# Adding the causal mask of a row-maximum pass on VectorE instead of TensorE

## The chip, the cores and the metric

The kernel runs on one core of a Trainium2 chip. The metric is the device time of one execution in microseconds (us). A core has five engines with a queue each: TensorE (PE in the profile; its weight loads are listed apart as PEld), VectorE (DVE), ScalarE (ACT), GpSimd (POOL) and SyncE (SP), which here issues the DMAs. Engines wait for each other through semaphores.

## The reference, cut to what matters

The reference is two transformer layers over `x` of shape (2, 1024, 1024): attention, a mixing layer, attention, and a layer with a mixture of experts. The change lies in the two attentions, which compute the same apart from how the rotary pairs are formed:

```python
scores = jnp.einsum('bqhd,bkhd->bhqk', q, k) / np.float32(np.sqrt(HEAD_DIM))
mask = jnp.triu(jnp.full((seq_len, seq_len), -jnp.inf, dtype=scores.dtype), k=1)
scores = scores + mask
attn = jax.nn.softmax(scores.astype(jnp.float32), axis=-1).astype(q.dtype)
out = jnp.einsum('bhqk,bkhd->bqhd', attn, v).reshape(bsz, seq_len, N_HEADS * HEAD_DIM)
```

There are 32 query heads of 32 dimensions and 8 key/value heads, so 8 groups of 4 query heads. The sequence is 1024 long.

## The kernel before

`attention` handles one layer. For each of 2 batches it normalises and transposes `x`, projects keys, values and queries, and then works through the 8 head groups. In each group it makes the scores twice.

The **first pass** only finds each query's largest score, since the softmax is taken relative to it. Its work is cut into 38 uses (`USES`), each of which fills up to one PSUM bank of 512 columns: 8 tiles of 128 queries (`qt`), against one or two chunks of 512 keys (`kc`). A use is marked `last` when it holds the diagonal block. Then its width `n` is 128, 256, 384 or 512, and the two narrow widths put 4 or 2 heads side by side in a bank. 16 uses are not `last` (one head, 512 columns each). 22 are: 2 of four heads, 4 of two heads, 8 of one head with 384 columns and 8 of one head with 512.

For a use, `row_scores` (TensorE) waits until the bank is free, issues a score matmul per head (L738) and, in a `last` use, a second matmul per head (L743) that adds a 128x128 mask onto the last 128 columns: identity times a bf16 tile `negmask`, which holds 0 on and under the diagonal and -1e30 above. `maximum` (VectorE, L597) waits for the scores, takes one reduction over the whole bank with a result per head into `mx`, and frees the bank. Two banks of `psh` are used in turn, by `bank_plan`, so a use's scores wait for the maximum two uses earlier. At the end (`MT`) the maxima are merged, transposed on TensorE and stored to DRAM, from where the next group's second pass takes them as a 97th row of the queries.

The **second pass** (`ST`, L789) makes the transposed scores per unit of 128 keys by up to 512 queries, ScalarE takes the exponential (L502), GpSimd zeroes what the mask hides (L436), and TensorE multiplies by values and by ones (`PV`, L809). `NORM` on VectorE takes a reciprocal (L641, 3.35 us) and multiplies.

The order on every engine is written out by `iteration`: in the body for group g the second pass of g is interleaved with the query projection for g + 2 (`P`, L717) and the first pass of g + 1 (`S`, spread over the units 1 to 9). TensorE executes in that order, and VectorE takes its part of the same order: the maxima, the rotation after a projection (L580 to L585), the low parts (L590, L551) and `NORM`. The first group's first pass stands in `prologue`, among projections. So each batch of each layer has one first pass in the prologue and seven in the bodies; the last group's body has none.

Around the change, from the iteration's order (each step is issued as it stands):

```
ST 2,0  ST 2,1  S0  PV 1,0  S1  PV 1,1  S2  ST 3,0  S3  ST 3,1  PV 2,0  S4  PV 2,1  S5 ...
```

Of the kernel before, what the change touches and what calls it, by code (L numbers as in the profile page):

```python
# [16 lines left out]
BF16 = mybir.dt.bfloat16  # L17
ALU = mybir.AluOpType
ACT = mybir.ActivationFunctionType
AX = mybir.AxisListType  # L20

P = 128
# [8 lines left out]
BANK = 512  # L31
# [6 lines left out]
MASKED = -1e30  # L38
# [31 lines left out]
USES = score_uses()  # L70
# [119 lines left out]
def attention(nc, sem, layer, x_in, wqkv, cos_in, sin_in, swap, oT_d):  # L190
# [7 lines left out]
    s = {n: sem(f"a{layer}_{n}") for n in (  # L198
        "const", "table", *(f"xf{i}" for i in range(NX_BUF)), *(f"xl{i}" for i in range(NX_AHEAD)), "stats", "pow", "z_ready", "zT_ready", "zT_hi", "zT_evac",
        "wl0", "wl1", "w_hi", "w_ready", "sh_ready", "sh_free", "roped", "q_hi", "q_lo", "v_ready",  # L200
        "k_out", "q_out", "qs00", "qs01", "qs10", "qs11", "ks0", "ks1", "mx_ready", "mT_ready", "m_out", "mr0", "mr1", "st_ready",
        "exp_done", "mask_done", "pv_done", "acc_copied", "norm_done", "vg_ready", "os0", "os1",
        "pool_turn", "sp_turn", "pe_turn")}
    x_first, x_loaded = [s[f"xf{i}"] for i in range(NX_BUF)], [s[f"xl{i}"] for i in range(NX_AHEAD)]
    w_loaded = (s["wl0"], s["wl1"])
    max_row, o_stored = (s["mr0"], s["mr1"]), (s["os0"], s["os1"])
# [15 lines left out]
    with ExitStack() as ctx:  # L222
        def sb(name, shape, dt=F32):
            return ctx.enter_context(nc.sbuf_tensor(f"a{layer}_{name}", shape, dt))

        ident = sb("ident", [P, P])
        identb = sb("identb", [P, P], BF16)
        negmask = sb("negmask", [P, P], BF16)
        ones = sb("ones", [P, HD])
        nhalf = sb("nhalf", [P, 1])  # L230
        cos = sb("cos", [P, S])
# [185 lines left out]
        def _(pool):  # L417
# [26 lines left out]
                    copy_v(b, g + 2, par)  # L444

            pool.memset(ident[:, :], 0.0)
            pool.memset(negmask[:, :], 0.0)
            pool.memset(ones[:, :], 1.0)
            pool.memset(nhalf[:, :], -0.5)
            pool.drain()  # L450
            for i in range(2):
# [1 line left out]
            pool.drain()  # L453
            pool.affine_select(out=ident[:, :], in_=ident[:, :], compare_op=ALU.not_equal, fill=1.0, base=0,
                               pattern=[[-1, P]], channel_multiplier=1)
            pool.affine_select(out=negmask[:, :], in_=negmask[:, :], compare_op=ALU.is_ge, fill=MASKED, base=0,
                               pattern=[[-1, P]], channel_multiplier=1)
            pool.drain()
            pool.tensor_copy(identb[:, :], ident[:, :])
            pool.drain().then_inc(s["const"], 1)  # L460
            for k in range(ST_):
                reciprocal_deviation(k, k)
# [85 lines left out]
        def _(dve):  # L548
# [42 lines left out]
                    .then_inc(s["q_lo"], 1)  # L591

            def maximum(u, at, k):
                qt, kc, n, heads, _ = USES[k]
                m = len(heads)
                dve.wait_ge(s["sh_ready"], u + 1)
                dve.tensor_reduce(mx_hq[kc][:, heads[0]:heads[0] + m, qt],  # L597
                                  psh[:, at, 0:m * n].rearrange("p (m n) -> p m n", n=n), AX.X, ALU.max)\
                    .then_inc(s["sh_free"], 1)

            def max_rows(u, at):

# [103 lines left out]
        def _(pe):  # L706
# [25 lines left out]

            def row_scores(u, where, par, k):
                _, at, prev = where
                qt, kc, n, heads, last = USES[k]
                pe.wait_ge(s["sh_free"], SH0 + u + prev + 1)
                for i, h in enumerate(heads):
                    mm = pe.matmul(psh[:, at, i * n:(i + 1) * n], qst[par][0:96, h, qt * P:(qt + 1) * P],  # L738
                                   kst[par][0:96, kc * BANK:kc * BANK + n], start=True, stop=not last,
                                   skip_group_check=True)  # L740
                    if last:

                        mm = pe.matmul(psh[:, at, (i + 1) * n - P:(i + 1) * n], identb[:, :], negmask[:, :],  # L743
                                       start=False, stop=True, skip_group_check=True)
                mm.then_inc(s["sh_ready"], 1)

            def transpose_max(n, u, where):
# [1133 lines left out]
```

## Time and profile before

| quantity | value |
|---|---|
| median of 3 runs | 3196.64 us (3193.96 to 3196.96) |
| span of the profiled execution | 3192.5 us |
| median less span | 4.1 us |
| TensorE busy | 2861.6 us, 90% |
| VectorE busy | 2039.7 us, 64% |
| ScalarE busy | 1004.8 us, 31% |
| GpSimd busy | 282.5 us, 9% |

The profiled execution has no time of its own beside its span; the runs' times also hold what lies ahead of the first and after the last instruction. In the rows, L738 is line 738 of the kernel, `a_psh<-a_kst,a_qst` is what an instruction writes and reads, x48 is a count, and `<-DVE a_mx` behind an idle time names what ended it. A matmul's booked time includes its way through the array, so neighbouring ones overlap.

### The profile page before, as it was taken

The page shows a single profiled execution, that of the slowest core. Times are in us where ns is not written, and L with a number is a line of the kernel's source. Part 1 is how long each engine was busy: PE and PEld are TensorE (multiplying, and loading weights), DVE is VectorE, ACT ScalarE, POOL GpSimd, SP SyncE. Part 2 cuts the span into 40 slices and gives each one's busy share as a digit, 9 for nine tenths or more (in the row PEclk, how much of TensorE's full clock was granted, in tenths as well). Part 3 has the DMA queues.
Part 4 walks back from the last instruction along what each step waited for, and adds up shares of the span by engine and source line. Part 5 has one row for each costly group of instructions (what it writes and reads, how often), then busy time and mean ns, then how long its engine had stood idle before and what let it go on. Part 6 is the DMA issues. An engine that isn't in the chain of part 4 may idle for free. (4 is left out here: it accounts for less than half of the span.)

```text
span 3192.5 us, 48849 instructions
## 1 busy us (share of the span) xinstructions
PE 2861.6 (90%) x16848; PEld 1854.1 (58%) x16848; DVE 2039.7 (64%) x3303; ACT 1004.8 (31%) x1549; POOL 282.5 (9%) x397
## 2 busy tenths in 40 slices
PE   7999998999999799752869999989999997897999
PEld 6555454655554488642656555546555553786887
DVE  7676677767776433588776766767677774324443
ACT  2234334224334411252521433433234334201000
POOL 1011011001110000000010001011011110001111
PEclk9999999999999899875979999999999999998999
DMA  4322222323121322000133213213313120544111
GB/s 154 91 62 86 62 61 80 111 63 101 54 81 51 124 84 75 0 0 0 79 132 116 75 53 87 69 55 103 104 53 100 53 80 20 193 138 152 67 63 43
DMA packets 121063, 253.16 MB, mean 79 GB/s; under 512 B 12720, under 2 KB 39728, under 8 KB 120880
## 3 DMA queue, kind: packets, MB, share of 16 engines
q1 hardware_dynamic: 120912, 251.03, 24.8%
q8 instruction: 109, 1.79, 0.2%
q14 instruction: 42, 0.34, 0.0%
HBM read 166.57 MB, written 84.41 MB: 79 GB/s over the span
## 5 line engine op out<-in xcount | busy, mean ns | idle before, releaser
L597 DVE TENSOR_REDUCE a_mx<-a_psh 128x1 f32<-128x512 f32 (+3 forms) x1216 | 773.2, 660 | 351.5 <-PE a_psh L743 236.8
L502 ACT ACTIVATE a_prob<-a_pst 128x1024 f32<-128x1024 f32 (+3 forms) x768 | 595.9, 816 | 823.3 <-PE a_pst L789 821.0
L738 PE MATMUL a_psh<-a_kst,a_qst 96*128 96x512 f32 (+3 forms) x1536 | 543.6, 404 | 9.4 <-DVE a_mx L597 3.4
L738 PEld LDWEIGHTS a_psh<-a_kst,a_qst 96*128 96x128 f32 x1536 | 287.4, 192 | 396.8 <-DVE a_mx L597 327.4
L789 PE MATMUL a_pst<-a_qst,a_kst 97*128 97x512 f32 (+2 forms) x1536 | 424.3, 377 | 46.6 <-issue 17.5
L809 PE MATMUL a_ppv<-a_prob,a_vg 128*32 128x512 f32 (+3 forms) x3072 | 333.7, 507 | 12.5 <-POOL a_prob L436 11.1
L789 PEld LDWEIGHTS a_pst<-a_qst,a_kst 97*128 97x128 f32 x1536 | 256.6, 196 | 138.6 <-issue 72.3
L809 PE MATMUL a_pden<-a_prob,a_ones 128*32 128x512 f32 (+3 forms) x3072 | 329.9, 502 | 0.0
L436 POOL TENSOR_SCALAR_AFFINE_SELECT a_prob<-a_prob 128x512 f32<-128x512 f32 x256 | 178.6, 698 | 1383.7 <-ACT a_prob L502 1383.7
L641 DVE RECIPROCAL a_dens<-a_dens 128x512 f32<-128x512 f32 x64 | 214.6, 3353 | 68.2 <-ACT a_dens L510 55.2
L743 PE MATMUL a_psh<-a_negmask,a_identb 128*128 128x128 bf16 x1024 | 228.7, 232 | 0.0
L717 PE MATMUL a_psh<-a_xT_hi,a_w_hi 128*128 128x512 f32 x416 | 178.2, 428 | 2.6 <-issue 2.0
L717 PE MATMUL a_psh<-a_xT_lo,a_w_hi 128*128 128x512 f32 x416 | 168.2, 404 | 0.0
L1371 PE MATMUL h_pout<-h_w,h_o 128*128 128x512 f32 x720 | 167.7, 392 | 0.3 <-DVE h_x L1248 0.3
L717 PE MATMUL a_psh<-a_xT_hi,a_w_lo 128*128 128x512 f32 x416 | 167.5, 403 | 0.0
L743 PEld LDWEIGHTS a_psh<-a_negmask,a_identb 128*128 128x128 bf16 x1024 | 99.8, 97 | 93.9 <-issue 53.4
L1371 PEld LDWEIGHTS h_pout<-h_w,h_o 128*128 128x128 f32 x720 | 134.1, 188 | 28.2 <-DMA h_wb<-in_w_branch 0.7
L717 PE MATMUL a_pst<-a_xT_hi,a_w_hi 128*128 128x512 f32 x352 | 142.4, 404 | 6.7 <-DVE a_swp L581 4.5
L717 PE MATMUL a_pst<-a_xT_hi,a_w_lo 128*128 128x512 f32 x352 | 137.5, 391 | 0.0
L717 PE MATMUL a_pst<-a_xT_lo,a_w_hi 128*128 128x512 f32 x352 | 137.5, 391 | 0.0
L1454 PE MATMUL h_pout<-h_w,h_dg 128*128 x256 | 67.7, 411 | 61.9 <-ACT h_dg L1220 45.8
L809 PEld LDWEIGHTS a_pden<-a_prob,a_ones 128*32 128x32 f32 x3072 | 71.7, 110 | 82.7 <-issue 73.5
(213 smaller groups left out, 3786.8 us busy)
## 6 DMA issues: line engine op xcount, KB each, us to landing
a_qst<-q SPq DMA_DIRECT2D x192, 256.0 KB, 4.5
a_wraw<-in_wqkv SPq DMA_DIRECT2D x52, 512.0 KB, 5.6
q<-a_stg_hi SPq DMA_DIRECT2D x64, 256.0 KB, 2.5
q<-a_stg_lo SPq DMA_DIRECT2D x64, 256.0 KB, 2.8
oT<-a_oT SPq DMA_DIRECT2D x64, 256.0 KB, 2.5
a_kst<-kT SPq DMA_DIRECT2D x96, 128.0 KB, 3.0
h_oraw<-oT SPq DMA_DIRECT2D x16, 512.0 KB, 4.1
h_x<-in_x SPq DMA_DIRECT2D x16, 512.0 KB, 4.7
```

The lines of the kernel that those rows point to most:

```text
L436: pool.affine_select(out=blk, in_=blk, compare_op=ALU.is_ge, fill=0.0, base=0, pattern=[[0, GH], [1, P]], channel_multiplier=-1)\
L502: act.activation(prob[k % 2][:, 2 * half:2 * half + 2, off:], pst[:, half, :, off:], ACT.Exp, scale=scale).then_inc(s["exp_done"], 1)
L597: dve.tensor_reduce(mx_hq[kc][:, heads[0]:heads[0] + m, qt], psh[:, at, 0:m * n].rearrange("p (m n) -> p m n", n=n), AX.X, ALU.max)\
L641: dve.reciprocal(dens[:, :], dens[:, :])
L717: mm = pe.matmul(bank(at), w[par][a][:, k, :], xT[x][:, k, c * BANK:(c + 1) * BANK], start=(i == 0), stop=(i == len(passes) - 1))
L738: mm = pe.matmul(psh[:, at, i * n:(i + 1) * n], qst[par][0:96, h, qt * P:(qt + 1) * P], kst[par][0:96, kc * BANK:kc * BANK + n], start=Tru ...
L743: mm = pe.matmul(psh[:, at, (i + 1) * n - P:(i + 1) * n], identb[:, :], negmask[:, :], start=False, stop=True, skip_group_check=True)
L789: mm = pe.matmul(pst[:, half, hh, off:], kst[par][0:97, ki * P:(ki + 1) * P], qst[par][0:97, 2 * half + hh, qc * BANK + off:(qc + 1) * BAN ...
L809: mm = pe.matmul(acc[h * HD:(h + 1) * HD, off:], lhs, prob[k % 2][:, h, off:], start=(ki == 0), stop=(ki == 4 * qc + 3), skip_group_check= ...
L1371: mm = pe.matmul(pout[:, half, :], o[:, par, a, k, :], w[:, b, k, half * BANK:(half + 1) * BANK], start=(i == 0), stop=(i == len(passes) - 1))
L1454: mm = pe.matmul(pout[:, par, i * C:(i + 1) * C], dg[par][:, i * (NS + 1) + n, :], rhs, start=(n == 0), stop=(n == NS), skip_group_check=True)
```

## The change

VectorE adds the mask. In a `last` use, `maximum` issues one `tensor_tensor_reduce` per head: it adds the tile `edge` to the scores, writes the sums back over the scores in PSUM, and delivers the largest sum. `edge` is a bf16 tile of 512 columns, zeros with the triangle in its last 128 columns, so that its last n columns fit a use of width n. The mask matmuls, `negmask` and the bf16 identity `identb` go, with a drain and a cast at set-up. The wait of a `last` use is taken by a semaphore step on VectorE (`dve_turn`) ahead of its instructions. Other uses keep their reduction.

```diff
+        edge = sb("edge", [P, BANK], BF16)
-        identb = sb("identb", [P, P], BF16)
-        negmask = sb("negmask", [P, P], BF16)
...
+            pool.memset(edge[:, :], 0.0)
-            pool.affine_select(out=negmask[:, :], in_=negmask[:, :], compare_op=ALU.is_ge, fill=MASKED, base=0,
-                               pattern=[[-1, P]], channel_multiplier=1)
-            pool.drain()
-            pool.tensor_copy(identb[:, :], ident[:, :])
+            pool.affine_select(out=edge[:, BANK - P:], in_=edge[:, BANK - P:], compare_op=ALU.is_ge, fill=MASKED,
+                               base=0, pattern=[[-1, P]], channel_multiplier=1)
...
             def maximum(u, at, k):
-                qt, kc, n, heads, _ = USES[k]
+                qt, kc, n, heads, last = USES[k]
                 m = len(heads)
                 dve.wait_ge(s["sh_ready"], u + 1)
-                dve.tensor_reduce(mx_hq[kc][:, heads[0]:heads[0] + m, qt],
-                                  psh[:, at, 0:m * n].rearrange("p (m n) -> p m n", n=n), AX.X, ALU.max)\
-                    .then_inc(s["sh_free"], 1)
+                if last:
+
+                    dve.sem_inc(s["dve_turn"], 1)
+                    for i, h in enumerate(heads):
+                        scores = psh[:, at, i * n:(i + 1) * n]
+                        part = dve.tensor_tensor_reduce(scores, scores, edge[:, BANK - n:], 1.0, 2 * MASKED,
+                                                        ALU.add, ALU.max, mx_hq[kc][:, h, qt:qt + 1])
+                else:
+                    part = dve.tensor_reduce(mx_hq[kc][:, heads[0]:heads[0] + m, qt],
+                                             psh[:, at, 0:m * n].rearrange("p (m n) -> p m n", n=n), AX.X, ALU.max)
+                part.then_inc(s["sh_free"], 1)
...
             def row_scores(u, where, par, k):
                 for i, h in enumerate(heads):
                     mm = pe.matmul(psh[:, at, i * n:(i + 1) * n], qst[par][0:96, h, qt * P:(qt + 1) * P],
-                                   kst[par][0:96, kc * BANK:kc * BANK + n], start=True, stop=not last,
+                                   kst[par][0:96, kc * BANK:kc * BANK + n], start=True, stop=True,
                                    skip_group_check=True)
-                    if last:
-
-                        mm = pe.matmul(psh[:, at, (i + 1) * n - P:(i + 1) * n], identb[:, :], negmask[:, :],
-                                       start=False, stop=True, skip_group_check=True)
                 mm.then_inc(s["sh_ready"], 1)
```

## Rows read from the trace of the kernel before

**Rows 1.** The page: busy time by engine, and the chain that ended last.

```profile
PE 2861.6 (90%) x16848; PEld 1854.1 (58%) x16848; DVE 2039.7 (64%) x3303; ACT 1004.8 (31%) x1549; POOL 282.5 (9%) x397
...
PE 8%; DVE 1%; DMA 0%; issue 0%; DVEq 0%; SPq 0%; ACT 0%; POOL 0%
```

**Rows 2.** Windows: two head groups, the maxima's stretch, a prologue's maxima.

```profile
core 0: us, PE busy (x) PEld busy (x) DVE busy (x) ACT busy (x) POOL busy (x), PEclk, DMA share, GB/s
173.00:229.00 56.00, 55.84 (x377) 29.80 (x369) 41.05 (x58) 22.30 (x31) 6.41 (x9) 1.00 0.26 75
229.00:292.00 63.00, 58.47 (x373) 32.15 (x369) 40.67 (x57) 22.63 (x31) 5.55 (x9) 0.95 0.23 66
188.60:227.50 38.90, 38.74 (x271) 19.25 (x268) 26.96 (x44) 16.44 (x23) 3.64 (x5) 1.00 0.27 73
78.00:111.00 33.00, 29.42 (x146) 19.90 (x145) 28.08 (x45) 2.12 (x2) 0.74 (x2) 1.00 0.24 72
```

**Rows 3.** Groups by line, 188.6 to 227.5: count | busy, mean ns | idle before.

```profile
L597 DVE TENSOR_REDUCE a_mx<-a_psh 128x1 f32<-128x512 f32 (+3 forms) x38 | 24.2, 660 | 11.6 <-PE a_psh L743 7.7 <-PE a_psh L738 3.7
L738 PE MATMUL a_psh<-a_kst,a_qst 96*128 96x512 f32 (+3 forms) x48 | 17.1, 406 | 0.2
...
L738 PEld LDWEIGHTS a_psh<-a_kst,a_qst 96*128 96x128 f32 x48 | 9.0, 192 | 13.3 <-DVE a_mx L597 11.3 <-issue 1.6
```

**Rows 4.** The page's costliest groups: the mask matmuls.

```profile
L743 PE MATMUL a_psh<-a_negmask,a_identb 128*128 128x128 bf16 x1024 | 228.7, 232 | 0.0
```

**Rows 5.** Timeline of TensorE's matmuls: start us, us, then the instruction.

```profile
188.66 0.73 PE L789 MATMUL a_pst<-a_qst,a_kst 97*128 97x256 f32 x4
189.22 0.22 PE L738 MATMUL a_psh<-a_kst,a_qst 96*128 96x128 f32 x1
189.29 0.23 PE L743 MATMUL a_psh<-a_negmask,a_identb 128*128 128x128 bf16 x1
...
189.48 0.23 PE L743 MATMUL a_psh<-a_negmask,a_identb 128*128 128x128 bf16 x1
...
196.14 0.34 PE L738 MATMUL a_psh<-a_kst,a_qst 96*128 96x384 f32 x1
196.33 0.23 PE L743 MATMUL a_psh<-a_negmask,a_identb 128*128 128x128 bf16 x1
196.37 0.71 PE L789 MATMUL a_pst<-a_qst,a_kst 97*128 97x512 f32 x2
196.91 0.40 PE L738 MATMUL a_psh<-a_kst,a_qst 96*128 96x512 f32 x1
...
197.32 0.43 PE L809 MATMUL a_ppv<-a_prob,a_vg 128*32 128x128 f32 x8
...
214.17 0.40 PE L738 MATMUL a_psh<-a_kst,a_qst 96*128 96x512 f32 x1
...
214.88 0.40 PE L738 MATMUL a_psh<-a_kst,a_qst 96*128 96x512 f32 x1
215.21 1.06 PE L809 MATMUL a_ppv<-a_prob,a_vg 128*32 128x512 f32 x8
```

**Rows 6.** Groups by line and shape, whole span: the reductions.

```profile
L597 DVE TENSOR_REDUCE a_mx<-a_psh 128x1 f32<-128x512 f32 x768 | 510.3, 688 | 204.4 <-PE a_psh L738 105.1 <-PE a_psh L743 92.5
...
L597 DVE TENSOR_REDUCE a_mx<-a_psh 128x1 f32<-128x384 f32 x256 | 136.1, 553 | 69.8 <-PE a_psh L743 67.0
L597 DVE TENSOR_REDUCE a_mx<-a_psh 128x2 f32<-128x512 f32 x128 | 88.1, 691 | 59.8 <-PE a_psh L743 59.8
...
L597 DVE TENSOR_REDUCE a_mx<-a_psh 128x4 f32<-128x512 f32 x64 | 44.1, 689 | 17.5 <-PE a_psh L743 17.5
```

**Rows 7.** Timeline of VectorE at the start and near the end of the stretch.

```profile
190.97 1.28 DVE L597 TENSOR_REDUCE a_mx<-a_psh 128x4 f32<-128x512 f32 x2
192.96 0.69 DVE L597 TENSOR_REDUCE a_mx<-a_psh 128x2 f32<-128x512 f32 x1 [0.71 <-PE a_psh L743]
...
222.87 1.29 DVE L597 TENSOR_REDUCE a_mx<-a_psh 128x1 f32<-128x512 f32 x2 [0.37 <-PE a_psh L738]
```

**Rows 8.** Short and two-source VectorE work: groups by line, then a timeline.

```profile
L1352 DVE SCALAR_TENSOR_TENSOR h_x<-h_w,h_m,h_x x128 | 56.3, 481 | 18.0 <-issue 18.0
L581 DVE LOAD_MASK_SELECT a_swp<-a_psh x52 | 0.7, 14 | 0.0
...
2980.26 0.16 DVE L1652 TENSOR_REDUCE e_sc<-e_ge 128x1 f32<-128x8 f32 x1 [1.06 <-ACT e_ge L1602]
2980.34 0.14 DVE L1653 TENSOR_SCALAR e_sc<-e_ge 128x1 f32<-128x1 f32 x1
```

**Rows 9.** Waits, 78 to 111 us: us in total, times, longest.

```profile
DVE a_mx L597 <- PE a_psh L743: 2.8, 10, 0.4
```

**Rows 10.** Timeline of the start: GpSimd's last set-up step and TensorE's first matmuls.

```profile
4.16 0.29 POOL L459 CAST a_identb<-a_ident 128x128 bf16<-128x128 f32 x1
...
8.82 1.97 PE L729 MATMUL a_pst<-a_ident,a_xin 128*128 128x128 f32 x8 [8.82 <-DVE a_xin L566]
```

More of the change, by code:

```diff
@@ L202, in attention @@
         "exp_done", "mask_done", "pv_done", "acc_copied", "norm_done", "vg_ready", "os0", "os1",
-        "pool_turn", "sp_turn", "pe_turn")}
+        "pool_turn", "dve_turn", "sp_turn", "pe_turn")}
     x_first, x_loaded = [s[f"xf{i}"] for i in range(NX_BUF)], [s[f"xl{i}"] for i in range(NX_AHEAD)]
@@ L446, in _ @@
             pool.memset(ident[:, :], 0.0)
-            pool.memset(negmask[:, :], 0.0)
+            pool.memset(edge[:, :], 0.0)
             pool.memset(ones[:, :], 1.0)
@@ L734, in row_scores @@
                 _, at, prev = where
-                qt, kc, n, heads, last = USES[k]
+                qt, kc, n, heads, _ = USES[k]
                 pe.wait_ge(s["sh_free"], SH0 + u + prev + 1)
```

## The prediction

> **What bounds the kernel now.** I read the busy shares first, then the stretches by window, then the waits inside one stretch, then the timeline. TensorE is busy 90% of the span, VectorE 64% [rows 1]. The chain that ended last only covers the expert layer at the end [rows 1], so it says nothing of the attention; that has to be read by window. One head group of the attention takes 56.0 us and TensorE is busy 55.84 of them; in the 38.9 us in which the row maxima of the next group are made it is busy 38.74, at a granted clock of 1.00, with VectorE busy 26.96 [rows 2]. So TensorE's queue sets the time there. The waits seem to say otherwise: weight loads of the scores stand 11.3 us behind the maxima [rows 3]. But a PE matmul row has only 0.2 us of idle before L738 in the same stretch [rows 3]: these loads wait while other matmuls run. VectorE has slack: it stood 11.4 us waiting for scores (7.7 and 3.7) [rows 3]. Every second group takes 63 instead of 56 us [rows 2]; the extra is around the jump of the loop, not among the maxima. The stretch runs 28 times (7 groups, 2 batches, 2 layers). The maxima of each batch's first group, 4 times, are made in the prologue, where VectorE is busy 28.08 of 33.0 us and TensorE 29.42 [rows 2].
>
> **What goes: 1024 mask matmuls.** They are booked at 228.7 us [rows 4], 0.23 each, but matmuls overlap and the price is the shift of the next start. Score (384 columns), mask and two 512-column matmuls of L789 take 196.91 - 196.14 = 0.77. An unmasked 512-column score with two of the same takes 214.88 - 214.17 = 0.71 [rows 5]. Four unmasked 256-column matmuls take 189.22 - 188.66 = 0.56, or 0.14 each [rows 5], against 0.71/3 = 0.235 for 512, so 128 columns are 0.05, and the unmasked 384 would take 0.66. The mask costs 0.11. Where a probability matmul (L809) follows, the pair takes 197.32 - 196.91 = 0.41 with a mask and 215.21 - 214.88 = 0.33 without [rows 5]: 0.08. Between the 128-column scores a pair takes 189.48 - 189.29 = 0.19 against 0.14, the shortest pitch seen: 0.05. By the written order 8 of the group's 32 masks stand before L809, 6 between short scores, 18 elsewhere: 8 x 0.08 + 6 x 0.05 + 18 x 0.11 = 2.9 us a group. Bounds: 1.1 us if only the 0.035 between a mask's start and the next start is given back (196.33 to 196.37 [rows 5]), and 2.9.
>
> **What VectorE gets.** The 16 unmasked reductions stay. The 22 masked ones (2 over four heads, 4 over two, 16 single; 8 of these of 384 columns) become 32, one a head. The columns are the same, 8 x (128 + 256 + 384 + 512) = 10240. From 688 ns at 512 and 553 at 384 [rows 6] a column costs 1.055 ns, so 10.8 us either way. What changes is the fixed part f of an instruction. Now the 22 are booked at 2 x 689 + 4 x 691 + 8 x 688 + 8 x 553 = 14.1 us, a fixed 0.15 each. No row shows the new instruction, and it must also deliver its running maximum, so I count a main part and a short readout. Main part: 0.15 alone; 0.07 if it starts under the tail of the one before (two reductions together last 1.29, one alone 0.69, so they start 0.60 apart) [rows 7]. Readout: the nearest row is a one-element operation that starts 0.08 after a short one when nothing drains between them (2980.26, 2980.34) and takes 0.14 to 0.16 alone [rows 8]. So f is 0.15 if both overlap and 0.24 if only the readout does; I take the middle, 0.20. Outer bounds: 0.08 (0.07 and a companion record like LOAD_MASK_SELECT's 0.014 [rows 8]) and 0.37. The latter is the two-source instruction L1352, 0.48 for 256 columns, so 0.21 fixed, and 0.16 of readout, the longer of the short ones [rows 8]. Per group VectorE then works 10.8 + 32f - 14.1 more: +3.1 us at 0.20.
>
> The Trainium skill ("VectorE: DVE Perf Modes", "Two Vector instructions with no wait between them") says that an operation that also writes out its accumulator is two instructions, the main one and a read. By this page f has two parts, as taken above; no row here shows the pair, and if the rule did not hold the sum would be that of the lower bound.
>
> **Who waits.** A score use may start on TensorE only when the maximum two uses earlier has freed its bank. I walk the uses of the stretch: each TensorE step keeps its length from the timeline less its mask, each maximum starts at the later of its scores and the end of the one before. At f = 0.20: VectorE comes free from the rotation at 190.97 [rows 7], late for use 0. Four heads of 128 columns take 4 x (0.135 + 0.20) = 1.34, now 0.69: free at 192.3. Use 2, which could start at 191.8 (192.22 less the masks before it), stands 0.54. Use 1 then ends near 193.25 (2 x 0.47), so use 3 stands 0.42, the exposed weight load of 0.1 included. Use 5 stands 0.09, and after that VectorE is ahead: the later uses come with an L809 step of 1 us between them. 1.05 us of the 2.9 go back, 1.86 stay: 28 x 1.86 = 52 us.
>
> The same walk at other f: 0.08 keeps 2.67 a group, 0.15 keeps 2.25, 0.24 keeps 1.50, 0.30 keeps 0.75, 0.37 loses 0.71.
>
> **The prologue.** VectorE's idle there is 33.0 - 28.1 = 4.9, of which 2.8 wait for masked scores [rows 9]. Work of 31.2 plus the other 2.1 of idle is 33.3: 0.3 us longer, four times +1. By the same sum f = 0.15 gives -5, 0.24 gives +6, 0.30 gives +14, 0.37 gives +23. At f = 0.08 VectorE would give 3.5 a time, but TensorE's own 6 x 0.05 + 26 x 0.11 = 3.2 caps it, about -12.
>
> **The rest at nothing.** Set-up loses a cast and a drain and fills a wider tile; POOL is done at 4.45 us and TensorE first needs it at 8.82 [rows 10], and 4.4 us of cover are far above one wider fill. [...] Queued behind a late maximum are the low parts and weight splits; their takers have several us. No DMA is moved. The row maximum comes 1.7 us earlier and its store with it, ahead of its use by the next group. TensorE's clock is 1.00 in the stretch and its gaps stay under 0.6 us, so I count no change.
>
> Sum at f = 0.20: -52 + 1 = -51. The profiled span is 3192.5, 4.1 below the median of 3196.6 of the runs; the difference is applied to the median: 3146.
>
> **Rivals.**
> 1. *The readout is dear, and VectorE becomes the bound.* At f = 0.30 the attention gives -21 and the prologue +14; break-even is f = 0.305. At 0.37 it is 20 + 23 = +43, 3240. For it: 0.15 for any one-element operation run alone [rows 8], and a first stretch where VectorE starts late. Against it: short operations 0.08 apart. The Trainium skill's rules for kernel authors (the same page, "Rules for kernel authors") speak for this rival: fewer operations, no fusing for speed; 22 become 32, each perhaps two. Chance 13%.
> 2. *Writing back into the bank it reads halves the rate.* The new instruction writes its sums over the scores; no row has VectorE writing PSUM. Columns cost twice: the walk loses 3.6 a group, 28 x 3.6 = 100, prologue (3.1 + 10.8 + 2.1 + 28.1 - 33.0) x 4 = +44, so +144, 3341. Against it: L1352 reads two f32 tiles and writes one in place at 0.48 for 256 columns [rows 8], full rate. Chance 8%. A rule of the Trainium skill ("Vector Engine (DVE) Microarchitecture Reference", "Points that are easy to get wrong") names a halving for this family with two non-bf16 SBUF sources; here one source is in PSUM and the mask is bf16, so by its letter it does not apply, and L1352, without an accumulator, does not show it.
> 3. *VectorE is hidden everywhere.* f = 0.08 gives 28 x 2.67 + 12 = 87, 3110; all of TensorE's saving would be 94, 3103. It asks for a free readout. Chance 8%.
> 4. *The mask was nearly free.* If only 1.1 us a group comes back, the walk keeps 0.54: -14, 3182. Against it: the pairs of [rows 5] have the same work behind them and differ in the mask alone. Chance 5%.
> 5. *Break-even* from f between 0.29 and 0.32: 5%.
>
> The forecast, f from 0.10 to 0.29, has the remaining 61%. Its own range is 3118 to 3187.
>
> **How the numbers follow.** A difference of 0.2%, 6.4 us, is about what can be told from no change. Faster: forecast, 3 and 4, 61 + 8 + 5 = 74%, less 2 for forecasts near its upper end, 72%. Same: 5 plus those 2: 7%. Slower: 1 and 2, 21%. The range runs from 3110 (free readout) to 3215 (f = 0.34). Left out are a full saving (2%), f above 0.34 (5%) and the halved rate (8%).
>
> **What would show it.** No L743 rows and 1024 VectorE instructions in place of 704. A group's TensorE busy time down by 2 to 3 us, groups of 54 rather than 56. TensorE idle before the score matmuls, 0.2 a stretch now, at about 1, all in its first 7 us. VectorE busy in the stretch 26.96 + 3.1 = 30. If new rows start more than 0.83 us apart at 512 columns (0.54 + 0.29), step "what VectorE gets" is wrong; if there is no idle and the gain is small, the mask's price was.

## The result, and the profile after

The changed kernel takes 3168.1 us (median of 4 runs, 3152.4 to 3174.8) against 3196.7 (3194.0 to 3197.0). The ratio is 0.991, 95% interval 0.9884 to 0.9935: faster by 28.5 us, where 51 was forecast. The four runs of the changed kernel lie 22 us apart, those of the kernel before 3; the shortest of them has the highest mean granted clock (0.938), the longest the lowest (0.930). The profiled execution has a span of 3167.0 us (before 3192.5), and its mean granted TensorE clock is 0.935 (before 0.947).

The page after, to set beside [rows 1, 4, 6]:

```profile
PE 2824.7 (89%) x15824; PEld 1810.8 (57%) x15824; DVE 2122.0 (67%) x4647; ACT 1003.6 (32%) x1549; POOL 282.8 (9%) x395
...
q8 instruction: 69, 1.13, 0.1%
q14 instruction: 90, 0.74, 0.1%
...
L599 DVE CUSTOM_DVE_ANT_0 a_psh<-a_psh,a_edge 128x128 f32<-128x128 f32 (+3 forms) x1024 | 486.8, 513 | 189.1 <-PE a_psh L743 181.8
...
L599 DVE DVE_READ_ACCUMULATOR2_ANT a_mx<- 128x1 f32 x1024 | 144.2, 141 | 0.0
```

The 1024 mask matmuls are gone (L743 is now the score matmul). Each of the 1024 new instructions has two records, a main part and a read of the accumulator. The Trainium skill ("VectorE: DVE Perf Modes", "Two Vector instructions with no wait between them") says the same of an operation that writes out its accumulator; the trace agrees, with 141 ns for the read.

To find where the time went I took the length of every head group, from one copy of the row maxima (L611, before L606) to the next. A batch has seven such lengths; between two batches lies one long interval with a prologue in it. In us:

```
before  61.9 55.8 63.2 55.8 61.9 55.8 52.6 | 133.3 | 61.9 55.7 55.8 55.8 55.8 55.8 51.3 | 685.7 | 61.8 55.7 63.5 55.8 64.0 55.8 53.0 | 133.1 | 61.9 55.7 55.8 55.8 55.8 55.8 51.4
after   60.9 53.7 60.2 53.7 61.2 53.7 49.3 | 137.4 | 58.4 53.6 60.3 53.6 57.1 53.6 50.8 | 689.8 | 61.0 53.6 60.3 53.7 61.2 53.6 48.8 | 136.0 | 59.4 53.6 61.4 53.7 60.3 53.7 50.4
```

The third and fifth length of each batch hold the passage through the jump of the loop over pairs of groups: 8 in all. The other steady groups went from 55.8 to 53.65, a gain of 2.1. The 8 behind a jump hold 52.9 us above a plain group in after, and held 29.5 before. The prologues lost too: 4.1, 4.1 and 2.9 us in the long intervals, and 1.0 in the first (its copy starts at 112.07 instead of 111.03). So: 28 groups x -2.1 = -59; jumps 52.9 - 29.5 = +23; prologues +12. That is -24, of -25.5 between the spans.

Windows of after, a plain group and one behind a jump, to set beside [rows 2]:

```profile
core 0: us, PE busy (x) PEld busy (x) DVE busy (x) ACT busy (x) POOL busy (x), PEclk, DMA share, GB/s
700.60:754.30 53.70, 53.19 (x342) 27.90 (x345) 43.70 (x100) 22.20 (x31) 6.44 (x9) 1.00 0.27 78
754.30:814.60 60.30, 57.74 (x341) 29.93 (x341) 43.31 (x99) 22.62 (x31) 5.91 (x9) 0.92 0.24 69
```

The two do the same work, yet the second has 4.5 us more of TensorE busy time, and its granted clock is 0.92. Here is VectorE's timeline behind the jump:

```profile
766.51 0.69 DVE L650 TENSOR_TENSOR a_oT<-a_pvs,a_dens 128x512 f32<-128x512 f32 x1
769.71 0.69 DVE L587 TENSOR_TENSOR a_stg_lo<-a_rot,a_stg_hi 128x512 fp32r<-128x512 f32 x1 [2.51 <-issue]
770.32 1.22 DVE L548 TENSOR_TENSOR a_w_lo<-a_wraw,a_w_hi 128x1024 fp32r<-128x1024 f32 x1
...
774.53 0.29 DVE L599 CUSTOM_DVE_ANT_0 a_psh<-a_psh,a_edge 128x128 f32<-128x128 f32 x1
```

"Issue" means that the profile shows nothing it waited for. Whole span, the waits of VectorE and then of TensorE in after:

```profile
DVE a_stg_lo L587 <- issue: 19.7, 8, 2.6
...
PE a_psh L743 <- DVE a_mx L599: 20.7, 42, 1.3
...
PE a_psh L743 <- DVE a_swp L578: 8.5, 8, 1.2
```

Eight waits (the first row), one at each jump, and none of them in before. Before had a different one, four times, on TensorE, which is its share of the 29.5 us. It is gone in after, where TensorE's program is shorter. The row of before:

```profile
PE a_pst L789 <- issue: 17.5, 4, 4.5
```

TensorE's timeline behind the jump in after:

```profile
773.12 0.50 PE L743 MATMUL a_psh<-a_kst,a_qst 96*128 96x256 f32 x2 [1.09 <-DVE a_swp L578]
...
775.67 0.50 PE L743 MATMUL a_psh<-a_kst,a_qst 96*128 96x256 f32 x2 [1.28 <-DVE a_mx L599]
...
778.12 1.08 PE L810 MATMUL a_pden<-a_prob,a_ones 128*32 128x256 f32 x8
...
786.07 1.94 PE L810 MATMUL a_ppv<-a_prob,a_vg 128*32 128x512 f32 x8
787.94 0.76 PE L743 MATMUL a_psh<-a_kst,a_qst 96*128 96x512 f32 x2
```

and the same steps in the plain group before it:

```profile
718.18 0.50 PE L743 MATMUL a_psh<-a_kst,a_qst 96*128 96x256 f32 x2
...
719.86 0.50 PE L743 MATMUL a_psh<-a_kst,a_qst 96*128 96x256 f32 x2 [0.39 <-DVE a_mx L599]
720.20 0.40 PE L790 MATMUL a_pst<-a_qst,a_kst 97*128 97x256 f32 x2
720.62 0.44 PE L743 MATMUL a_psh<-a_kst,a_qst 96*128 96x384 f32 x1
...
722.16 0.64 PE L810 MATMUL a_pden<-a_prob,a_ones 128*32 128x256 f32 x8
...
726.64 1.07 PE L810 MATMUL a_ppv<-a_prob,a_vg 128*32 128x512 f32 x8
727.63 0.73 PE L743 MATMUL a_psh<-a_kst,a_qst 96*128 96x512 f32 x2
```

Read three things here. TensorE stands 1.09 + 1.28 us against 0.39. Then eight 512-column matmuls take 787.94 - 786.07 = 1.87 us against 0.99. The granted clock from 778 to 788 us is 0.50: this is the lower level of its clock (1.2 in place of 2.4 GHz). From the L810 at 778.12 to the L743 at 787.94 it takes 9.8 us, in the plain group 5.5 (722.16 to 727.63). So of the 6.6 us that this group is longer, 2.0 are idle time and 4.35 half-speed matmuls.

The other seven groups behind a jump show the same two parts. TensorE idles 2.2 to 2.5 us in each of the eight (0.3 to 0.4 in a plain group), some 16 us more in all; beyond a plain group's 53.2 us it is busy 36.6 us more in all, between 1.6 us (57.1 long, granted clock 0.97) and 5.7 (61.2 to 61.4 long, clock 0.89). So some two thirds of the 52.9 us are half-speed matmuls.

### The profile page after: what moved, and what is told of

Same layout as the page of the kernel before. It is cut to its first block and busy times, and to the rows that moved or that the text cites. A ratio compares the mean times of both kernels' runs of the same rounds, so it can differ in the third digit from the quotient of the medians.

```text
span 3167.0 us, 48845 instructions
## 1 busy us (share of the span) xinstructions
PE 2824.7 (89%) x15824; PEld 1810.8 (57%) x15824; DVE 2122.0 (67%) x4647; ACT 1003.6 (32%) x1549; POOL 282.8 (9%) x395
## 3 DMA queue, kind: packets, MB, share of 16 engines
q8 instruction: 69, 1.13, 0.1%
## 5 line engine op out<-in xcount | busy, mean ns | idle before, releaser
L599 DVE CUSTOM_DVE_ANT_0 a_psh<-a_psh,a_edge 128x128 f32<-128x128 f32 (+3 forms) x1024 | 486.8, 513 | 189.1 <-PE a_psh L743 181.8
L743 PE MATMUL a_psh<-a_kst,a_qst 96*128 96x512 f32 (+3 forms) x1536 | 527.0, 404 | 40.2 <-DVE a_mx L599 20.7
L743 PEld LDWEIGHTS a_psh<-a_kst,a_qst 96*128 96x128 f32 x1536 | 263.4, 193 | 480.0 <-DVE a_mx L599 224.9
L790 PE MATMUL a_pst<-a_qst,a_kst 97*128 97x512 f32 (+2 forms) x1536 | 414.0, 372 | 28.0 <-DMA a_qst<-rowmax 10.7
L602 DVE TENSOR_REDUCE a_mx<-a_psh 128x1 f32<-128x512 f32 x512 | 343.5, 688 | 74.5 <-PE a_psh L743 67.5
L810 PE MATMUL a_ppv<-a_prob,a_vg 128*32 128x512 f32 (+3 forms) x3072 | 341.4, 518 | 13.2 <-POOL a_prob L435 11.4
L790 PEld LDWEIGHTS a_pst<-a_qst,a_kst 97*128 97x128 f32 x1536 | 278.5, 200 | 128.5 <-issue 55.5
L810 PE MATMUL a_pden<-a_prob,a_ones 128*32 128x512 f32 (+3 forms) x3072 | 335.2, 509 | 0.0
L1372 PEld LDWEIGHTS h_pout<-h_w,h_o 128*128 128x128 f32 x720 | 134.1, 188 | 28.5 <-DMA h_wb<-in_w_branch 0.9
L599 DVE DVE_READ_ACCUMULATOR2_ANT a_mx<- 128x1 f32 x1024 | 144.2, 141 | 0.0
L810 PEld LDWEIGHTS a_pden<-a_prob,a_ones 128*32 128x32 f32 x3072 | 73.4, 112 | 106.0 <-issue 100.3
```

The costliest lines, as they stand in the source:

```text
L599: part = dve.tensor_tensor_reduce(scores, scores, edge[:, BANK - n:], 1.0, 2 * MASKED, ALU.add, ALU.max, mx_hq[kc][:, h, qt:qt + 1])
L602: part = dve.tensor_reduce(mx_hq[kc][:, heads[0]:heads[0] + m, qt], psh[:, at, 0:m * n].rearrange("p (m n) -> p m n", n=n), AX.X, ALU.max)
L790: mm = pe.matmul(pst[:, half, hh, off:], kst[par][0:97, ki * P:(ki + 1) * P], qst[par][0:97, 2 * half + hh, qc * BANK + off:(qc + 1) * BAN ...
L810: mm = pe.matmul(acc[h * HD:(h + 1) * HD, off:], lhs, prob[k % 2][:, h, off:], start=(ki == 0), stop=(ki == 4 * qc + 3), skip_group_check= ...
L1372: mm = pe.matmul(pout[:, half, :], o[:, par, a, k, :], w[:, b, k, half * BANK:(half + 1) * BANK], start=(i == 0), stop=(i == len(passes) - 1))
```

## The experiments

Theories, as the expectations name them. **A**: VectorE's instructions behind the loop's jump come late, TensorE then idles, and its clock falls. **B**: the mask was worth less than forecast. **C**: the new instructions' own length costs. **D**: the read of the accumulator or the write back costs a fixed amount. **E**: the wait at the jump comes from the kind of instruction, not from their number. **F**: lateness itself costs, not the clock. **G**: closer packing of the scores costs. **H**: another engine's loop has a part. The kernel before took 3194.2, 3193.3, 3194.8 and 3193.3 us (medians of 9, 7, 9 and 9 runs) beside e1 to e4, e5 to e8, e9 to e11 and e12.

**e1: no mask at all.** The kernel before, without the mask matmuls.

```diff
-                                   kst[par][0:96, kc * BANK:kc * BANK + n], start=True, stop=not last,
+                                   kst[par][0:96, kc * BANK:kc * BANK + n], start=True, stop=True,
-                    if last:
-                        mm = pe.matmul(psh[:, at, (i + 1) * n - P:(i + 1) * n], identb[:, :], negmask[:, :],
-                                       start=False, stop=True, skip_group_check=True)
```

> The kernel before with the mask matmuls left out and nothing put in their place: the row maximum is then taken over masked keys too (an upper bound of the true maximum, so the softmax is shifted by more). VectorE's program stays that of before. Theory A (the changed kernel's gain is eaten by VectorE standing for instructions after the loop's jump, which drops TensorE's clock): VectorE has no such wait here, a plain group takes 55.8 - 2.9 = 52.9 us, jump groups lose their extra as TensorE's program is shorter, prologues give 2 to 3 each: 3085 to 3110 us. Theory B (a mask is worth less than I counted, about 2.1 us a group): plain groups of 53.7, and 3125 to 3140 us.

Measured 3078.7 us, ratio 0.9638 (0.9623 to 0.9652). Plain groups take 52.6, and those behind a jump the same. The mask matmuls cost 55.8 - 52.6 = 3.15 us a group, so B falls. With neither wait at the jump, those groups cost nothing extra. The time is below A's range of 3085 to 3110: the mask is worth more than the 2.9 us that A took.

**e2 and e3: the loop over pairs of groups written out**, in the kernel after (e2) and in the kernel before (e3), on all engines.

```diff
-            with eng.Fori(0, NG // 2 - 1) as j:
+            for j in range(NG // 2 - 1):
                 for par in range(2):
```

> The changed kernel with the loop over pairs of head groups written out, so no engine jumps between groups; the work is the same. Theory A: the 8 groups behind a jump now take 57.1 to 61.4 us and the others 53.65, 53 us in all; without jumps all take 53.7, so 3110 to 3120 us, VectorE's 19.7 us of waits for nothing that the profile shows ahead of the low part gone. Theory C (the new instruction makes VectorE late in those groups by its own length): the time stays within 10 us of 3168.

> The kernel before with the same loop written out. Its groups behind a jump hold 29.5 us more than the plain ones (four of them, with TensorE's own wait of 4.4 us each). Theory A: that goes, 3165 to 3170 us, and the changed kernel written out is 1.6 to 1.8% faster than this one, twice the gain measured with loops. Theory C: this one gains as well, but the gap between the two written-out kernels stays at 0.9%.

e2 takes 3108.1 us, ratio 0.9739 (0.9724 to 0.9754), e3 3159.9, ratio 0.9897 (0.9881 to 0.9912). Written out, the change is worth 51.8 us (3159.9 to 3108.1). All steady groups of e2 take 53.4 to 53.8, all of e3 55.8 to 55.9. The long intervals are 3.4, 2.0 and 3.9 us longer in e2. So the jump is where the loss beyond the forecast lies. Both times are below the ranges named (by 2 and 5 us), their difference of 1.6% is the one that A names.

**e4: both masks.** The changed kernel with the mask matmuls put back in as well.

```diff
-                qt, kc, n, heads, _ = USES[k]
+                qt, kc, n, heads, last = USES[k]
...
+                    if last:
+                        mm = pe.matmul(psh[:, at, (i + 1) * n - P:(i + 1) * n], identb[:, :], negmask[:, :],
+                                       start=False, stop=True, skip_group_check=True)
```

> The changed kernel with the mask matmuls of before put back on TensorE, so the mask is added twice: VectorE's part of the change alone. Theory A: plain groups at 55.8 to 56.0 us, as TensorE's queue sets them and VectorE's extra work is hidden, and groups behind a jump dear, as VectorE's waits stay: 8 x 6.6 - 29.5 = +23, 3215 to 3230 us. Theory C: every group pays, plain ones take 57 or more, 3240 or more.

3222.1 us, ratio 1.0105 (1.008 to 1.013). Plain groups take 55.8, as before the change: with TensorE 3.15 us slower, VectorE's extra work is hidden in full. The groups behind a jump take 62.9 to 65.4 in the first batch of a layer and 57.8 in the second, where the same wait of VectorE costs 2.0 us at a granted clock of 1.00; A had 6.6 for every one. TensorE's wait is back (17.7 us, 4 times) beside VectorE's (14.9 us, 6 times).

**e5: one reduction a head.** e1 with 48 plain reductions a group in place of 38. The mask is left out.

```diff
-                dve.tensor_reduce(mx_hq[kc][:, heads[0]:heads[0] + m, qt],
-                                  psh[:, at, 0:m * n].rearrange("p (m n) -> p m n", n=n), AX.X, ALU.max)\
-                    .then_inc(s["sh_free"], 1)
+                for i, h in enumerate(heads):
+                    part = dve.tensor_reduce(mx_hq[kc][:, h:h + 1, qt],
+                                             psh[:, at, i * n:(i + 1) * n].rearrange("p (m n) -> p m n", n=n),
+                                             AX.X, ALU.max)
+                part.then_inc(s["sh_free"], 1)
```

> The kernel without a mask in the row maximum (as e1), but with one reduction per head, 48 a group in place of 38: the number of instructions of the changed kernel without its readouts and without the second operand. Theory A (a plain group of the changed kernel takes 1.0 us more than one of e1 because VectorE's fixed part per instruction, 0.115 us with the readout, is paid 32 times instead of 22): plain groups at 52.9 to 53.4 us, no wait of VectorE for instructions, 3085 to 3100 us. Theory D (the readout, or writing back into PSUM, costs the 1.0 us): 52.6 to 52.7 a group and 3079 to 3083 us.

3080.6 us, ratio 0.9646 (0.963 to 0.9662), plain groups 52.9. Ten more plain instructions cost 0.3 us a group; the groups lie at the lower end of A's range (52.9 to 53.4) and the time in D's, so the number of instructions is a part of the 1.0 us and not all of it. No wait at the jump appears (43 packets on q14, as in e1).

**e6: filler.** e1 with three semaphore steps on VectorE ahead of each of the 22 diagonal reductions. They do no work; the mask is left out.

```diff
+                for _ in range(3 * last):
+                    dve.sem_inc(s["dve_turn"], 1)
```

> The kernel of e1 with three semaphore steps on VectorE's queue ahead of each of the 22 reductions of a diagonal block, 66 a group; the changed kernel has 64 instructions a group more there (22 steps, 10 more mains, 32 readouts). They do no work. Theory A (the length of VectorE's program is what makes it stand after the loop's jump): waits for nothing that the profile shows ahead of the low part, 2 to 3 us in each of the 8 groups behind a jump, the scores late behind them, TensorE's clock down there, and these groups 5 to 8 us longer than the other 20, which stay at 52.6 to 52.9: 3115 to 3140 us. Theory E (the wait comes from the new instruction itself, its table or its kind, after a jump): no such wait, 3079 to 3085 us.

3135.3 us, ratio 0.9819 (0.9803 to 0.9835). The wait is there though no new instruction is, so E falls. VectorE's waits in e6, and its instruction queue over the whole span:

```profile
DVE a_stg_lo L590 <- issue: 19.2, 8, 2.6
```

```profile
q14 instruction: 90, 0.74, 0.1%
```

These are after's own numbers (19.7 us, 8 times; 90 packets). The groups behind a jump take 55.3 to 55.6, 2 us above e6's plain ones, so some 16 of the 57 us that e6 is slower than e1. Its plain groups went from 52.6 to 53.3: the filler also costs something by itself.

The expectation had these groups 5 to 8 us longer and TensorE's clock down, and that part was missed. TensorE idles 1.8 to 2.1 us in each of them, is busy 53.2 to 53.4 (53.1 in a plain group of e6), and its granted clock stays at 1.00. So the wait by itself costs 2 us a jump, in e6 eight times and in e4 four times; what the groups of after take beyond that goes with the fall of the clock.

**e7: the weight split later**, in the changed kernel. It is one of the instructions between the wait and the rotation. The edit moves it three units, not the two that the expectation names.

```diff
-        after[steps[0][0]] += [("WS", 0)]
+        after[steps[3][0]] += [("WS", 0)]
```

> The changed kernel with the split of the next weights (1.2 us on VectorE, 1.1 on ScalarE) moved two units later in every engine's order, out of the way of the rotation ahead of the first maxima. VectorE's wait after the jump stays. Theory A (the wait costs mostly by TensorE's clock, which falls after two idle stretches of 1.1 and 1.3 us in 4 us): the idle goes down by about 1.2 us or more, the clock stays at 1.00 in most groups behind a jump, and they fall from 57 to 61 to about 54 to 56 us: 3120 to 3145 us. Theory F (the lateness itself costs, the clock does not): the groups gain at most the 1.2 us each, 3158 to 3168 us.

3233.2 us, ratio 1.0124 (1.0107 to 1.0141): outside the ranges of both theories. Plain groups grew to 55.7 to 58.4. VectorE's timeline shows why:

```profile
741.88 0.14 DVE L599 DVE_READ_ACCUMULATOR2_ANT a_mx<- 128x1 f32 x1
743.71 1.23 DVE L548 TENSOR_TENSOR a_w_lo<-a_wraw,a_w_hi 128x1024 fp32r<-128x1024 f32 x1 [1.69 <-ACT a_w_hi L475]
```

The split now stands among the maxima and waits for ScalarE's half of it, and the maxima and then the scores wait behind it. The run says nothing of the jump.

**e8: no mask, written out** (e1 and e2 together; the mask is left out).

> The kernel of e1 (no mask in the row maximum) with the loop over pairs of groups written out. Theory A: e1's groups behind a jump already take 52.6 us like the others, so there is nothing to win but small waits: 3070 to 3082 us. Were jumps costly in themselves, with short programs too, it would gain 20 us or more.

3078.2 us, ratio 0.9635 (0.9619 to 0.9651), the same as e1. Writing the loop out is worth nothing where no engine waits at the jump.

**e9 and e10: the scores start later**, in the changed kernel: from the middle of unit 1 (e9) and from unit 2 on (e10).

```diff
-        window = [step for unit in steps[1:10] for step in unit]
+        window = [step for unit in steps[1:10] for step in unit][2:]     # e9
+        window = [step for unit in steps[2:10] for step in unit]         # e10
```

> The changed kernel with the 38 score uses spread over the steps from the middle of unit 1 on (before: from its start), so the first use is issued some 2.5 us later and the others move closer together. Nothing is left out. Theory A (the 2.5 us that VectorE waits behind each jump make it late for the first scores, TensorE idles, and its granted clock falls for some 10 us): VectorE's wait in front of the low part stays at 8 times 2.5 us, but TensorE no longer idles at the first scores, the groups behind a jump come down from 57 to 61 us towards 54 to 56, and the time is 3115 to 3145. Rival F (VectorE's lateness itself costs, wherever the scores begin): no change, 3160 to 3175. Rival G (the tighter packing of the later scores costs more than the start gives): plain groups grow past 54.5 us and the time is over 3180.

> The changed kernel with the score uses spread over units 2 to 9 instead of 1 to 9: the first use is issued some 5 us later. Nothing is left out. Theory A: as for the half unit, with no idle time at all in front of the first scores, 3110 to 3140 if the tighter packing is free; with plain groups of up to 55 us the time is 3140 to 3170. Rival F: 3160 to 3175 with plain groups unchanged at 53.7. Rival G: over 3180.

3162.3 us, ratio 0.9903 (0.9887 to 0.9919), and 3208.0, ratio 1.0035 (1.0021 to 1.0048). Theory A's expectation failed in both. e9's time lies in F's range. By e4 and e6 lateness itself costs 2 us a jump; what e9's groups take beyond that goes with the clock again (0.97 in those of 57 us, 0.89 in those of 62). In e9 the plain groups stay at 53.8, those behind a jump at 57 to 62, and TensorE's idle time there has only moved by a use:

```profile
770.14 0.51 PE L743 MATMUL a_psh<-a_kst,a_qst 96*128 96x256 f32 x2 [0.24 <-DVE a_swp L578]
772.71 0.50 PE L743 MATMUL a_psh<-a_kst,a_qst 96*128 96x256 f32 x2 [2.06 <-DVE a_mx L599]
```

0.24 + 2.06 = 2.3 us, against 1.09 + 1.28 = 2.4 in after. The first four uses are still issued within a few us, and with two banks the third waits for VectorE however late the first one starts. In e10 the plain groups are 55.4 to 55.8: the closer packing costs 1.8 us a group (G). This leaves A as a place (the jump), and shows that moving the scores within the order is no cure.

**e11: short chunks without the mask.** The changed kernel, but the new instruction only at 512 columns. That keeps 8 of a group's 32 and makes 14 wide reductions of the other 24; the expectation's counts of them (40, and 16 of 48) are wrong. The mask is left out of the shorter chunks.

```diff
-                if last:
+                if last and n >= BANK:
```

> The changed kernel with the masking maximum kept only where a chunk has 512 columns; the shorter diagonal chunks (20 of 38 uses have none of them, 14 of them do) are reduced without a mask, in the wide form of the kernel before. So part of the masking is left out of the row maximum. The 40 short masking instructions of a group become 14 wide ones. Theory C (what the change keeps the plain group from gaining in full, 53.65 against 52.65 us without masks, lies in the short instructions at the first uses, where VectorE sets the pace): plain groups fall to 52.7 to 52.9, and the program is shorter, so the groups behind a jump fall too: 3080 to 3100. Theory D (a fixed price of each masking instruction, wherever it stands): plain groups lose in proportion, 16 of 48 instructions stay, 53.0 to 53.2, and the time is 3100 to 3130.

3082.9 us, ratio 0.9653 (0.964 to 0.9667). All steady groups take 52.8 to 52.9, also behind a jump. So what the change leaves of the mask's 3.15 us goes with the short instructions. C and D are not told apart by it: with the right counts, D asks for 8/32 of 1.05, 0.26 us above the 52.6 of e1, and 0.2 to 0.3 is measured. (The timelines of after and e1, below, speak for C.) The wait at the jump is gone, and q14 in e11 shows:

```profile
q14 instruction: 45, 0.36, 0.0%
```

**e12: the loop written out on VectorE alone**, the other four engines keep theirs. Nothing is left out.

```diff
+            if written_out:
+                for j in range(NG // 2 - 1):
+                    for par in range(2):
+                        group(body, b, j * 2 + par, j, par, u0 + (j * 2 + par) * U_IT)
...
-                over_groups(b, dve, group, last)
+                over_groups(b, dve, group, last, True)
```

> The changed kernel with the loop over pairs of head groups written out on VectorE alone; the other four engines keep their loop. Nothing is left out. Theory A, in its sharper form (what costs is that VectorE's instructions behind its own loop jump come late, and nothing on another engine): no wait of VectorE in front of the low part of the keys, groups behind a jump at 53.4 to 53.9 us as the others, and 3105 to 3125 in all. Rival H (the loop of TensorE, ScalarE or SyncE has a part in it): groups behind a jump stay above 55 us and the time is 3130 to 3170.

3109.9 us, ratio 0.9741 (0.9728 to 0.9755), the same as e2. All steady groups take 53.3 to 53.6. H falls: what costs is VectorE's own jump.

**Where the missing instructions were.** The traffic of the instruction queues can be read by window. From 800 to 945 us the kernels are in the second batch of the first layer, past the first of its two jumps. In before, e1 and e11 no packet of q8 or q14 moves in that window; in after, and likewise in e4 and e6 (6 packets each):

```profile
q14 instruction: 6, 0.05, 0.1%
```

And in the wait itself, between 767.20 and 769.71, one piece of 8 KB arrives. The window from 767 to 768 of after:

```profile
DMA packets 1, 0.01 MB, mean 8 GB/s; under 512 B 0, under 2 KB 0, under 8 KB 0
...
q14 instruction: 1, 0.01, 3.2%
```

The wait at 881.1 to 883.5 has one too (881.5 to 882). It is so in all eight: VectorE's first work behind the jump starts 1.95 to 2.14 us after that packet of q14 does, and in e6 1.94 to 2.20 us after it. TensorE's four waits in before end 2.64 to 2.72 us after a packet of q8. So VectorE's loop, once longer, is loaded again on every trip, and behind the jump the engine waits for the load. The packet itself takes 0.3 to 0.5 us; what the rest of the time goes to is not shown.

The same reading says why before waits only in the first batch of a layer. From 229 to 410 us, in the first batch's loop, 14 packets of q8 move; from 770 to 936 us, in the second's, none. The two batches are two copies of the code, and why one copy is held and the other not stays open. Packets alone cost nothing: e12, written out, has 3 on q14 from 800 to 945 us and no wait.

The Trainium skill ("Runtime: NRT & Kernel Launch", "Instruction fetch mechanics") describes this: fetching runs ahead in sequence only, and a taken branch to a target no longer held stalls the engine until it is fetched; it gives this as a reason why kernels prefer to be written out. The traces agree, at 2.3 to 2.6 us a jump, and so does e12. The page's blocks of 16 KiB do not fit everywhere: q8's packets are 1.13 MB / 69 = 16.4 KB, q14's 0.74 MB / 90 = 8.2 KB. That q8 carries TensorE's program and q14 VectorE's is worked out from the times above and from which program grew (e6, e11, e12), not shown by a label.

## Why the prediction was right, and by how much not

It was right in sign and mechanism: 28.5 us faster, inside its range of 3110 to 3215, above its point of 3146. That it lies in the range is in part luck: the upper half of the range was there for a dear readout, which did not come, and held a loss at the jumps and in the prologues that no step had. By its steps:

**TensorE sets the time, and the mask costs 2.9 us a group.** Right. e1 measures 3.15.

**What VectorE gets: f = 0.20.** Too dear. VectorE's timeline in a plain group of after:

```profile
718.71 0.29 DVE L599 CUSTOM_DVE_ANT_0 a_psh<-a_psh,a_edge 128x128 f32<-128x128 f32 x1
718.92 0.14 DVE L599 DVE_READ_ACCUMULATOR2_ANT a_mx<- 128x1 f32 x1
718.92 0.33 DVE L599 CUSTOM_DVE_ANT_0 a_psh<-a_psh,a_edge 128x128 f32<-128x128 f32 x1
719.17 0.14 DVE L599 DVE_READ_ACCUMULATOR2_ANT a_mx<- 128x1 f32 x1
...
721.88 0.56 DVE L599 CUSTOM_DVE_ANT_0 a_psh<-a_psh,a_edge 128x384 f32<-128x384 f32 x1
722.36 0.14 DVE L599 DVE_READ_ACCUMULATOR2_ANT a_mx<- 128x1 f32 x1
722.42 0.57 DVE L599 CUSTOM_DVE_ANT_0 a_psh<-a_psh,a_edge 128x384 f32<-128x384 f32 x1
```

The next main part starts together with the read of the one before, or 0.06 us behind it where a new use and its turn step come between (722.36, 722.42). The pitch is 0.25 us at 128 columns and 0.54 at 384; less the columns (0.135, 0.405) that is f = 0.115 to 0.135. Rivals 1 (dear readout) and 2 (half rate) are refuted, the second by the 384-column pitch, which is that of one pass at full rate.

**Who waits: 1.05 us given back.** Right in sum, but by luck: two errors cancel. With f = 0.12 the walk would give some 0.45 back. Set the plain group above beside the same steps of e1:

```profile
742.76 0.50 PE L738 MATMUL a_psh<-a_kst,a_qst 96*128 96x256 f32 x2
...
743.98 0.50 PE L738 MATMUL a_psh<-a_kst,a_qst 96*128 96x256 f32 x2
...
744.55 0.40 PE L738 MATMUL a_psh<-a_kst,a_qst 96*128 96x384 f32 x1
...
750.54 1.06 PE L805 MATMUL a_ppv<-a_prob,a_vg 128*32 128x512 f32 x8
```

From the first pair on, after is later by (719.86 - 718.18) - (743.98 - 742.76) = 0.46 us at use 2, by 0.65 at use 3 and by 0.68 at the L810 (726.64 against 750.54). The walk had 0.54 and 0.96. Near the end of the stretch, at the four 384-column uses of the last but one tile, another 0.27 goes, where the walk had VectorE ahead. Together 0.95 of the 1.05 between 53.65 and 52.6.

The other error is that the walk lets a maximum start as soon as its scores are there. The third 384-column score in after and its masked maximum, then in e1 and its reduction:

```profile
722.73 0.44 PE L743 MATMUL a_psh<-a_kst,a_qst 96*128 96x384 f32 x1
723.37 0.57 DVE L599 CUSTOM_DVE_ANT_0 a_psh<-a_psh,a_edge 128x384 f32<-128x384 f32 x1 [0.32 <-PE a_psh L743]
```

```profile
746.63 0.44 PE L738 MATMUL a_psh<-a_kst,a_qst 96*128 96x384 f32 x1
747.11 2.04 DVE L597 TENSOR_REDUCE a_mx<-a_psh 128x1 f32<-128x384 f32 x3 [0.37 <-PE a_psh L738]
```

The masked maximum starts 0.20 us after the booked end of its scores (723.17), the plain reduction 0.04 (747.07). In e6, with three semaphore steps between wait and reduction, it is 0.33 (763.73 to 764.06), so a step costs about 0.1 where VectorE was idle. Of the 1.05 us, ten more instructions are 0.3 (e5), and 22 steps some 0.2, an estimate from the 0.7 us of e6's 66; no run takes the turn steps alone out of the changed kernel. The group then gained 2.1, forecast 1.86: 28 times that is -59 in place of -52.

**The prologue: +1.** Too low: about +12 with the loop, and e2 is 9 us longer than e3 there. The first two prologues of after have the same two large stalls in front of their scores (1.15 and 0.51 us). The first costs +1.0 at a granted clock of 1.00. In the second the clock falls, which the step on the clock excluded. From first maximum to copy it is 35.2 us (607.00 to 642.22) against 31.9 in before (619.22 to 651.15). A window of the second prologue, after:

```profile
615.00:625.00 10.00, 8.34 (x27) 5.70 (x27) 8.30 (x20) 0.26 (x1) 0.00 (x0) 0.79 0.15 53
```

The windows around it in before all have 1.00.

**The rest at nothing. This is the step that failed.** It went through the set-up, the low parts and the DMAs, and said of TensorE's clock "I count no change". It left out the size of VectorE's program. That grows by 64 instructions a group: 10 more maxima, 32 reads and 22 turn steps. e6's filler is 66 a group, and both kernels show 90 packets on q14 and the wait. The added instructions that e5 (10) and e11 (16) keep bring no wait. The hint stood in [rows 2]: a group behind the jump took 63 us at clock 0.95. The prediction read that as "around the jump of the loop, not among the maxima" and set it aside. It was the one place where the size of a program already cost 4.2 to 4.5 us four times, on TensorE. The change took that away and put a wait of 2.5 us eight times on VectorE, which reaches TensorE as 2.4 us of idle time and, since the clock falls behind it, as 6.6 us in all at 754 to 814. Net +23. With the loop written out, the change gives 51.8 us (e3 to e2), the forecast's 51: its sum holds where its missing term does not apply, again with help from errors that cancel (a steady group gives 2.4 there, not 1.86, and the prologues take some 9, not 1).

**What would show it.** No mask rows, 1024 new instructions in place of 704, groups of 54: as said (53.65). VectorE is 2.7 busier a group (43.70 against 41.05 [rows 2]), forecast 3.1. TensorE's idle time ahead of the scores, forecast near 1 us, is 0.4 in a plain group; the rest hides between matmuls, in rows that count as busy. Rivals 3 and 4 fall with f and e1; 5 did not occur.

What stays open: how much program VectorE holds (between e11's and after's, 16 and 64 instructions a group above e1's), and what tips the clock: in e6 and half of e4 TensorE idles 1.7 to 2.1 us behind the jump and the clock stays, in after 2.2 to 2.5 us and it falls each time, for longer or shorter. The sum of idle time alone does not decide it: one group of e10 (2399.9 to 2457.3 us) idles 3.5 us and keeps 1.00.

The fastest kernels are e1 and e8, 3078 us, without the mask. A larger row maximum cancels in the softmax, as long as the exponentials do not underflow, and the second pass masks the probabilities (L436 in these kernels) anyway. Of those with the whole mask, e2 and e12 are the fastest, 3108 and 3110.

## What to carry to other kernels

Before moving work between engines inside a loop, count the instructions that each engine's loop body gains and loses, semaphore steps too, and look in the profile for idle time put down to issue behind the jump, and for packets on the instruction queues inside the loop: together they say whether a body still fits (in a loop written out packets move too, without a wait). Where it does not, write the loop out on that one engine. And price a wait of the matmul engine with what follows it: here 2 us of idle time a jump were followed by 1.6 to 5.7 us more in half-speed matmuls in the changed kernel, and by none in e6.

## What the runs showed of the hardware

- The read of an accumulator on VectorE is booked at 141 ns but overlaps the next instruction in full; a masked maximum with its result costs 0.115 to 0.135 us from start to start beside its columns, where the plain reduction costs 0.60 - 0.54 = 0.06 at 512 columns [rows 7].
- A semaphore step between VectorE's wait and the next instruction costs about 0.1 us where VectorE was idle (e6: 0.33 us from scores to reduction with three steps, 0.04 in e1 with none).
- VectorE writes back into the PSUM bank that it reads at full rate: 0.54 us from start to start at 384 columns.
- A short bf16 matmul with its weights, between f32 ones, costs 3.15 us / 32 = 0.10 us, where its record says 0.23 [rows 4].
- VectorE's waits behind a jump measured 2.3 to 2.6 us in after, e6 and e9, and end 1.9 to 2.2 us after an 8 KB packet on q14; TensorE's in before measured 4.2 to 4.5 and end 2.6 to 2.7 us after a 16 KB packet on q8.
- The same wait of VectorE (TensorE idle some 2 us) was followed by a granted clock of 1.00 in all 8 jump groups of e6 and of 0.89 to 0.97 in all 8 of after.
